# A fused attention and mixture-of-experts kernel: lookups, weight loads and first row transposes at the first seam put in another order, masks and one table load moved

## The reference, cut to what matters

```python
xn = _layernorm(x)
x = x + _L0_attn_ref(xn, ...) + _L0_ffn_ref(xn, ...)   # linear attention, 16 heads; SiLU experts, width 176, and shared expert
xn = _layernorm(x)
x = x + _L1_attn_ref(xn, ...) + _L1_ffn_ref(xn, ...)   # causal linear attention, 8 heads; GELU experts, width 512

# layer 0, one expert e for the tokens routed to it
hg = jnp.einsum('th,ehi->eti', xf, wg)
hu = jnp.einsum('th,ehi->eti', xf, wu)
eo = jnp.einsum('eti,eih->eth', jax.nn.silu(hg) * hu, wd)

# layer 1, the part that the moved selections belong to
mask = jnp.tril(jnp.ones((n, n), q.dtype))
energy = jnp.einsum('bhnd,bhmd->bhnm', q, k) * mask
out = jnp.einsum('bhnm,bhmd->bhnd', energy, v)
```

## Time and profile before

| | |
|---|---|
| median of 3 runs | 897.45 us (894.57 to 899.02) |
| the profiled execution, its own time | 900.08 us |
| its span in the profile | 898.5 us |
| PE busy | 827.5 us, 92% of the span |
| DVE, POOL, ACT busy | 700.3, 623.8, 581.1 us |
| layer 0 experts begin (first L913) | 241.28 us |
| layer 1 experts begin | 636.8 us |

### The profile page before, as it was taken

The page is one execution under the profiler, slowest core; times in us unless marked ns, Lnnn a source line. Parts: engine busy times, 40 slices in busy tenths (PEclk is TensorE's granted clock), DMA queues, the critical chain, the costliest instruction groups (busy, mean ns, idle before and its releaser), DMA issues.

```text
span 898.5 us, 22649 instructions
## 1 busy us (share of the span) xinstructions
PE 827.5 (92%) x7937; PEld 737.8 (82%) x7937; DVE 700.3 (78%) x1812; ACT 581.1 (65%) x1190; POOL 623.8 (69%) x599
## 2 busy tenths in 40 slices
PE   5789989999899989998898889898999999999996
PEld 3678878889799989986665666566899999999995
DVE  6787788987577987897889998999765566567776
ACT  5756465545366667768887777665776666666660
POOL 4157777777005788785888888888877777777662
PEclk9999999999999989999999999999999999999998
DMA  9799998116659997972111111113766555678976
GB/s 264 236 372 357 357 353 296 53 54 192 216 165 274 319 304 225 288 226 78 42 42 37 37 41 42 44 42 121 288 186 213 176 173 186 198 236 268 290 248 206
DMA packets 130995, 173.98 MB, mean 194 GB/s; under 512 B 15810, under 2 KB 85954, under 8 KB 130628
## 3 DMA queue, kind: packets, MB, share of 16 engines
q1 hardware_dynamic: 96864, 124.43, 42.6%
q0 software_dynamic: 16640, 34.37, 11.9%
q10 hardware_dynamic: 17380, 13.73, 5.1%
HBM read 93.64 MB, written 80.97 MB: 194 GB/s over the span
## 4 chain that ended last, share of the span: by engine, by line
PE 48%; DVE 26%; issue 7%; POOL 6%; ACT 5%; SPq 5%; DMA 3%; DVEq 0%; ACTq 0%; POOLq 0%
PE pair L977 14%; PE pair L913 5%; PE pair L915 5%; PE pair L914 5%; POOL sent L2204 4%; PE pair L944 3%; PE pair L822 3%; DVE a_en L1718 2%; PE pair L733 2%; DVE X L1655 2%; DVE stats_t L1266 2%; SPq L618 2%; ACT a_rows L1845 2%; SPq L590 1%; PE pair L1101 1%
## 5 line engine op out<-in xcount | busy, mean ns | idle before, releaser
L2204 POOL DMA_INDIRECT sent<-a_rows,slot x224 | 224.0, 1000 | 68.1 <-issue 64.5
L2215 POOL DMA_INDIRECT ex_joined<-outs,slot x128 | 135.5, 1059 | 88.9 <-DMA outs<-ex_tile_out 50.5
L913 PE MATMUL pair<-ex_x_hi,ex_w_hi 128*128 128x256 f32 x497 | 146.5, 295 | 0.2 <-issue 0.2
L915 PE MATMUL pair<-ex_x_hi,ex_w_lo 128*128 128x256 f32 x497 | 140.4, 282 | 0.0
L914 PE MATMUL pair<-ex_x_lo,ex_w_hi 128*128 128x256 f32 x497 | 140.3, 282 | 0.0
L2306 POOL DMA_INDIRECT back<-ex_tile_out,slot x104 | 113.9, 1096 | 36.8 <-issue 26.5
L977 PE MATMUL pair<-ex_down_all,ex_hid 128*128 x1136 | 133.3, 276 | 0.5 <-issue 0.3
L977 PEld LDWEIGHTS pair<-ex_down_all,ex_hid 128*128 128x128 f32 x1136 | 129.7, 192 | 2.3 <-issue 2.3
L2019 ACT ACTIVATE ex_hid<-pair,ex_stage 128x256 f32<-128x256 f32 x284 | 107.5, 491 | 6.8 <-PE pair L915 3.4
L1881 ACT ACTIVATE ex_w_hi<-ex_stage 128x768 fp32r<-128x768 f32 (+1 forms) x72 | 67.4, 937 | 52.4 <-DMA ex_stage<-in_experts 52.4
L913 PEld LDWEIGHTS pair<-ex_x_hi,ex_w_hi 128*128 128x128 f32 x497 | 94.8, 191 | 0.6 <-issue 0.6
(11 more groups left out here) (269 smaller groups left out, 2025.7 us busy)
## 6 DMA issues: line engine op xcount, KB each, us to landing
outs<-v_heads SPq DMA_DIRECT2D x8, 4352.0 KB, 37.7
ex_stage<-in_experts SPq DMA_DIRECT2D x72, 322.0 KB, 3.5
ex_stage<-in_experts SPq DMA_DIRECT2D x72, 320.0 KB, 5.0
ex_tile_in<-sent SPq DMA_DIRECT2D x72, 128.0 KB
outs<-ex_tile_out SPq DMA_DIRECT2D x71, 128.0 KB
ex_joined<-back ACTq DMA_DIRECT2D x15, 512.0 KB, 5.8
ex_tile_in<-sent SPq DMA_DIRECT2D x54, 132.0 KB
X<-in_x SPq DMA_DIRECT2D x16, 256.0 KB, 5.0
```

Of the source, the lines that this page charges most:

```text
L913: pe.matmul(o[:, of_half], wh, x_hi[i % 2][:, of_half], start=True, stop=False)
L915: m = pe.matmul(o[:, of_half], wl, x_hi[i % 2][:, of_half], start=False, stop=True)
L2204: pool.indirect_dma_start(out=sent[layer], out_offset=bass.IndirectOffsetOnAxis(ap=slot_i[layer][k][:, s, j:j + 1], axis=0), in_=rows[laye ...
L2215: pool.indirect_dma_start(out=joined[g % NJOIN][:, j, k, :], out_offset=None, in_=outs, in_offset=bass.IndirectOffsetOnAxis(ap=slot_i[0][k ...
```

## The change

Four edits.

- SP looks up tiles 0 and 1 and loads their weights, and those of tile 2, ahead of `all_sent(0)`. The rows of tiles 0 and 1 follow it at once. The weights of tiles 3, 4, 5 and of 6 with 7 come behind the rows of tiles 1, 2, 3 and 4.
- PE transposes the rows of tile 0 behind the first of the four blocks of down matmuls of the last group, and those of tile 1 behind the third.
- POOL's two selections of a step come ahead of transfers 1 and 3, in place of behind them.
- ACT does a GELU on 8 numbers before the last two groups' leftovers of layer 1 attention, into a buffer that is free.

```diff
@@ sync_program
-            for n in range(NSTAGE[0]):
+
+            def first_weights(n):
                 if n < NSTAGE[1]:
                     sp.wait_ge(send_dma[((n + 1) * 2 * W0COLS - 1) // (ST * ROW)], SEND16)
                 else:
                     sp.wait_ge(xT_lo_here, NG)
-                load_weights(0, n, look_up(0, n)[1])
+                found = look_up(0, n)
+                load_weights(0, n, found[1])
+                return found
+
+            first_tiles = [first_weights(n) for n in range(2)]
+            first_weights(2)
             all_sent(0)
...
                 if n < NTILES:
-                    firsts, experts = look_up(0, n)
+                    firsts, experts = first_tiles[n] if n < 2 else look_up(0, n)
...
                     if n >= NSTAGE[0]:
                         load_weights(0, n, experts)
+                    if 1 <= n <= NIN:
+                        for m in {1: (3,), 2: (4,), 3: (5,), 4: (6, 7)}[n]:
+                            first_weights(m)
@@ tensor_program, output0
-                if e == NG - 1:
-                    rows_to_columns(0, 0, 3)
-                    rows_to_columns(0, 1, 6)
                 for i in range(GT):
+                    if e == NG - 1 and i == 1:
+                        rows_to_columns(0, 0, 3)
+                    if e == NG - 1 and i == 3:
+                        rows_to_columns(0, 1, 6)
                     for c in range(3):
@@ scalar_program
+            act.wait_ge(q1_max, NG)
+            act.activation(e1[0][0:1, 0:8], ident[0:1, 0:8], ACT.Gelu)
             squares(NG - 2)
@@ pool_program
                 transfer(0)
-                transfer(1)
                 if old and not masked_by_dve(e):
                     mask_energies(e, 0)
+                transfer(1)
                 transfer(2)
-                transfer(3)
                 if old and not masked_by_dve(e):
                     mask_energies(e, 1)
+                transfer(3)
```

## The result

The changed kernel takes 892.06 us (median of 12 runs, 887.46 to 895.64) where the kernel before takes 898.14 on the same chip (12 runs, 894.57 to 900.71): a ratio of 0.9922, 95% interval 0.9906 to 0.9939, or 7.0 us less (5.5 to 8.4). The two medians alone differ by 6.1; the ratio is worked out from all the runs. The forecast was 892.6. The profiled execution of the changed kernel took 887.88 us, 4.2 under its median; that of before, 900.08, was 2 above its own.

The account below looks back on a forecast made before the run. PE, busy 92% of the span, was taken as the bound, idling for late tile rows. Terms 4.8 (rows and PE order) + 0 (selections) + 0 (table), off the median 897.45, gave 892.6 us; range 889.0 to 896.3.

Parts of the forecast that it names:

- The seam: Start of the layer 0 experts: rows of tiles 0 and 1 arrive earlier, PE's holes and low clock go, 4.8 us gained.
- the sum of the four parts: Before the first expert product: first hole 1.86, second 1.45, stretched transposes 0.44, down matmuls at lower clock 1.1; 4.85 us.
- What is late next: Expert tiles after the first two: rows of tile 2 and weights of tile 3 arrive in time, 4.8 us carried through.
- the slower rival: Expert tiles 2 to 5: weights between row transfers make rows late, 4.9 us slower, 902.3 us; chance 0.04.
- L = 233: SP's release from its wait for the sends at 233, from where the slack of tiles 2 to 5 is gone.
- Selections, 0: POOL's 28 selections, moved one transfer up: gain at most 0.75 us, loss at most 0.3, taken as 0.
- The rival with richer selections: Layer 1 attention: earlier selections loosen several of POOL's steps; 6.3 us gained in all, 891.1 us; chance 0.12.
- Table, 0: ACT's GELU table load of 1.28 us, moved from 639.64 to before 626.97: gain between 0 and 0.3 us, taken as 0.
- The idle time named as its cover: ACT's idle stretch of 4.07 us before 626.97, into which the GELU table load was to move.
- From the first expert product to the end, 657 us unchanged: Sign of being right: everything after the first expert product takes as long as before, 657 us.
- my own bound: Sign of being wrong: the time from first expert product to the end changes by more than 1.5 us either way.
- the likeliest case: The forecast itself, whole kernel: a gain of 4 to 5.5 us, own range 891.5 to 894; chance 0.62.

Follow-up runs that it names:

- seam alone: SP's new order and PE's new order at the first seam, without moved selections or table load, against the kernel before: 893.75 against 898.63 us, ratio 0.9949.

## Why the prediction was right, and where it was not

**The seam, 4.8.** Right, in size and in its steps. SP's release was taken as 228 and is 227.97. The first expert product comes at 236.86, not 236.43, only because PE reaches the stretch 0.44 us later in this execution. PE finds both tiles' rows, the clock stays at the upper of its two levels, and the stretch is shorter by 4.86, where the sum of the four parts gave 4.85. The seam alone measures 4.6 (2.9 to 6.3).

**What is late next: nothing.** No PE wait for tile 2 or 3 appears; their transposes come at 239.10 and 243.47, 2.24 us and 6.61 us behind the first product, as the earlier trace rows has 2.24 and 6.61 between 241.28, 243.52 and 247.89. The weights between the rows are free, and the slower rival had no ground: it needed L = 233.

**Selections, 0 (bounds +0.75 and -0.3).** The time doesn't speak against it (2.2 us less to 1.8 more alone, an interval wider than the bounds), the reasoning fails. The step that failed: I asked only who waits for a selection, and who a selection waits for. A selection also stops an engine that has nothing to do with it, and that shows as longer instructions of DVE and never as a wait. So its bound on the gain was wrong in the steps, 3.5 to 4.3 us in nine of them. The rival with richer selections (6.3 in all, 891.1) had the sign and a wrong cause, POOL's looser steps. The two predicted details are there: PE's wait of 0.75 for the first selection is gone, and the one behind it, 0.51, has grown to 0.91. No selection of the changed kernel waits for a copy; in the run of the selections alone three do.

**Table, 0.** It was not run alone, so no run gives its time. In the changed kernel's trace:

```profile
609.70 1.28 ACT L2162 ACT_TABLE_LOAD   x1
611.00 0.21 ACT L2162 ACTIVATE a_e<-consts 1x8 f32<-1x8 f32 x1
613.78 0.60 ACT L2111 ACTIVATE a_sq<-pair 128x512 f32<-128x512 f32 x1 [2.57 <-DVE a_uo L1741]
```

1.28 + 0.21 of the 4.07 us of idle time are used, and 2.57 are left. The idle time named as its cover is the one that takes it.

**From the first expert product to the end, 657 us unchanged.** Wrong between the profiles: 886.4 - 236.86 = 649.5, 7.7 less. By my own bound that had to be looked into. In the profile of the seam alone it is 892.5 - 236.64 = 655.9, within the bound, but as the sum of two differences: the layer 0 experts are 3.6 us shorter there and layer 1 attention 2.1 longer. Of the 7.7, 3.0 lie in layer 1 attention, where the steps are shorter. The other 4.7 lie in the layer 0 experts, where no edit acts; 3.2 of them are one hole at tiles 21 and 22, 9.99 us from transposes to transposes in the profile of before and 6.75 after, with the clock of before behind it at

```profile
333.00:340.00 7.00, 6.90 (x36) 6.90 (x37) 4.22 (x14) 3.04 (x5) 5.45 (x6) 0.58 0.68 232
```

and at 1.00 in each of the other three executions. The layer 0 experts take 172.1 us in the profile of before and 168.4, 167.4 and 167.4 in the seam alone, the changed kernel and the selections alone, so it is that one execution that stands out. The kernel before does not always lose this: its 17 timed runs beside the selections alone have granted clocks of 0.989 to 0.995 over the span, and times of 901.05 down to 894.02 us.

**The time and the gain.** The time was hit closer than the gain, and that part is luck. 892.6 is 0.5 us from the measured 892.06; but it starts from 897.45, a median of three runs that lies 0.7 below that of the twelve, and the gain it takes off, 4.8 (4 to 5.5 in the likeliest case), lies below the measured 7.0 and outside its interval, 5.5 to 8.4. What is right is the mechanism and the size of the largest term; some 2 us of the gain the prediction doesn't have.

**The sum.** Seam alone 4.6 and selections alone 0.2 make 4.8; the whole change measures 7.0 (5.5 to 8.4). The intervals are wide enough for no gap at all. The profile offers a reason for one (the changed kernel kept the shorter steps because its clock did not fall and its POOL was not late: PE waited 0.61 us for `X` at the second seam and not 3.33), but one execution of each can't show that it is so in most. This stays open.

## What to carry to other kernels

When an operation moves, look not only for who waits for it, but for what runs beside it: list each neighbour's duration with and without overlap, in PSUM and SBUF forms apart. A long GpSimd selection over SBUF belongs beside VectorE work that reads PSUM, or beside none; whether another GpSimd operation holds anything is worth a small program of its own. Transfers that fill the queues are best issued behind the first small ones that something waits for, and here PE, finding its data at once, kept its clock besides; but such a gain exists only where the consumer is early enough to meet the hole. And set the difference of two profiles against that of the medians before explaining it: of the 12.2 us here 6.1 belonged to the two single executions (5.2 against the ratio's 7.0).

## What the hardware showed that I had not expected

- A selection of 1.1 us on GpSimd holds VectorE instructions that read SBUF, with two inputs (3.28 to 8.34 us for twelve) and with one (1.72 to 7.18), and leaves alone those with a PSUM input (7.27) and a reduction with one SBUF input (0.28). Powers on 128 x 8 numbers, 1.6 us each, hold nothing.
- The clock falls behind one stop of PE and not behind the same stop in another execution: behind 0.88 and 0.77 us of idle time in the tenth step it is 0.53 or 0.59 in two profiles and 1.00 in two.
- Two of four chips run the same program in 1034 to 1048 us in place of 898, with PE idle for reasons that the profile calls "issue" (18.4 us in front of the layer 1 down products alone in the profile of the kernel before, 0.3 on a chip of the case). An edit without effect on one kind of chip costs 1.6 to 1.7% on the other. What sets these chips apart I did not find.
